# Ranks behind the second transposition, deviations on ScalarE, the first rows on its queue, weights issued sooner

## The reference, cut to what matters

```python
def _ln(v, axis, eps): return (v - mean(v, axis)) / sqrt(var(v, axis) + eps)

# x: (8 images, 64 channels, 16, 16); 256 positions per image
xn  = _ln(x, axis=1, eps=1e-6)
kq  = w_kq @ xn + b_kq                        # 32 channels
v   = w_v @ xn + b_v
att = softmax(kq.T @ kq, axis=-1)             # 256 x 256 per image
x   = x + w_o @ (att @ v) + b_o

t   = tokens(x)                               # 2048 tokens of 64
n   = _ln(t, axis=-1, eps=1e-5)
p   = softmax(n @ router_w.T)                 # 8 experts
top2 = top_k(p, 2), its two shares normalised to 1
y_e = (silu(n @ w1[e].T) * (n @ w3[e].T)) @ w2[e].T    # 682 hidden
out = t + sum over the two chosen experts of share * y_e
```

## Time and profile before

| | |
|---|---|
| three runs | 178.60, 179.76, 181.26 us |
| profiled execution | 177.17 us, span 175.4 us |
| busy, share of the span | PE 81%, PEld 68%, DVE 57%, ACT 41%, POOL 49% |
| granted TensorE clock, mean | 0.942 |
| DMA | 33.00 MB, 188 GB/s on average |
| largest lines | `up` 52.0 us of matmuls in each of its two rows, `down` 28.8 us, `multiply` 33.7 us, row scatters 31.4 us (32 of 980 ns), result scatters 37.7 us (39 of 967 ns) |

### The profile page before, as it was taken

One profiled execution on the slowest core, in us unless ns is written; L12 is line 12 of the kernel. 1 busy time (PEld: TensorE's weight loads), 2 busy tenths in 40 slices (PEclk: granted clock), 3 DMA queues, 4 the chain that ended last, 5 costly groups with the idle time before them and its releaser, 6 DMA issues.

```text
span 175.4 us, 4915 instructions
## 1 busy us (share of the span) xinstructions
PE 142.0 (81%) x1697; PEld 119.7 (68%) x1697; DVE 99.8 (57%) x372; ACT 71.2 (41%) x141; POOL 85.8 (49%) x114
## 2 busy tenths in 40 slices
PE   1489969590892596996699999999999999985672
PEld 1357746370561495895598999999999989874262
DVE  1626756858739857589357474637364736443050
ACT  2347664512430144262153545454545445443011
POOL 2695223877773772577653353525262626266000
PEclk9999999999579569999699999999999999999699
DMA  4999400001781692179697969596969881000345
GB/s 120 322 288 279 110 0 11 23 15 34 234 338 35 151 392 83 43 251 344 206 381 215 396 199 373 174 356 194 325 207 348 275 327 49 13 30 15 95 156 120
DMA packets 19893, 33.00 MB, mean 188 GB/s; under 512 B 7691, under 2 KB 13100, under 8 KB 19868
## 3 DMA queue, kind: packets, MB, share of 16 engines
q1 hardware_dynamic: 16732, 29.55, 52.1%
q0 software_dynamic: 2272, 2.35, 4.0%
q10 hardware_dynamic: 864, 0.79, 1.4%
HBM read 25.55 MB, written 7.13 MB: 186 GB/s over the span
## 4 chain that ended last, share of the span: by engine, by line
issue 31%; POOL 29%; PE 17%; DMA 8%; ACT 5%; DVE 5%; SPq 1%; POOLq 1%; ACTq 0%; DVEq 0%
POOL ys L383 20%; POOL xs L374 9%; PE psum L1055 4%; ACT probs L466 3%; DMA xs<-xrows,pos 2%; DMA y_in<-ys 2%; PE psum L1126 2%; PE psum L940 2%; PE psum L929 2%; PE psum L919 1%; DVE xrows L643 1%; DMA ys<-y_out,y_row 1%; DMA proj<-projections 1%; DMA x_in<-xs 1%; PE psum L1034 1%
## 5 line engine op out<-in xcount | busy, mean ns | idle before, releaser
L383 POOL DMA_INDIRECT ys<-y_out,y_row x39 | 37.7, 967 | 43.3 <-DVE y_out L848 34.1
L1055 PE MATMUL psum<-x_cols,weights 64*128 64x128 f32 x390 | 52.0, 288 | 3.5 <-DMA weights<-experts 3.3
L1055 PEld LDWEIGHTS psum<-x_cols,weights 64*128 64x128 f32 x390 | 48.1, 197 | 7.5 <-issue 5.4
L1057 PE MATMUL psum<-x_cols,weights 64*128 64x128 f32 x390 | 52.0, 288 | 0.0
L836 DVE TENSOR_TENSOR hid<-psum,act_sb 128x512 f32<-128x512 f32 (+1 forms) x50 | 33.7, 678 | 30.6 <-ACT act_sb L515 30.3
L1057 PEld LDWEIGHTS psum<-x_cols,weights 64*128 64x128 f32 x390 | 48.1, 197 | 0.0
L515 ACT ACTIVATE act_sb<-psum 128x512 f32<-128x512 f32 (+1 forms) x50 | 29.3, 586 | 29.8 <-PE psum L1055 29.8
L374 POOL DMA_INDIRECT xs<-xrows,pos x32 | 31.4, 980 | 18.4 <-DVE xrows L643 10.0
L1082 PE MATMUL psum<-hid,weights 128*64 128x128 f32 x468 | 28.8, 276 | 0.0
L1082 PEld LDWEIGHTS psum<-hid,weights 128*64 128x64 f32 x468 | 25.9, 137 | 1.8 <-DVE hid L836 0.3
L929 PE MATMUL psum<-ident,probs 128*128 128x128 f32 x32 | 6.6, 340 | 8.9 <-ACT probs L466 8.7
(11 more groups left out here) (150 smaller groups left out, 182.1 us busy)
## 6 DMA issues: line engine op xcount, KB each, us to landing
weights<-experts SPq DMA_DIRECT2D x39, 565.0 KB, 6.1
xs<-zeros SPq DMA_DIRECT2D x4, 1040.0 KB, 12.3
x_in<-xs SPq DMA_DIRECT2D x39, 32.5 KB
ys<-y_out,y_row POOLq DMA_INDIRECT x39
xs<-xrows,pos POOLq DMA_INDIRECT x32, 2.9
y_in<-ys ACTq DMA_DIRECT2D x2, 256.0 KB, 4.6
y_in<-ys SPq DMA_DIRECT2D x2, 256.0 KB, 4.3
x_sb<-x_tok SPq DMA_DIRECT2D x1, 384.0 KB, 3.6
```

Source lines behind the costliest of these rows:

```text
L383: nc.gpsimd.indirect_dma_start(ys, bass.IndirectOffsetOnAxis(ap=y_row[:, j:j + 1], axis=0), y_out[:, i % RING, h, :], None).then_inc(y_sca ...
L1055: first_ = nc.tensor.matmul(H1_BANK[g % 2][:, src], weights[0:C, slot, P * s:P * (s + 1)], x_cols[0:C, i % 2, src], start=True, stop=True)
L1057: second_ = nc.tensor.matmul(H3_BANK[g % 3][:, src], weights[C:P, slot, P * s:P * (s + 1)], x_cols[C:P, i % 2, src], start=True, stop=True)
```

## The change

- **Deviations.** POOL's two helpers go. ACT computes exp(-1/2 ln(variance + eps)) in two small activations, from a table set that has both functions: `inverse_deviations(k)` in two batches (pair 0; pairs 1 to 3 together) and `t_deviation(p)` for the second normalisation. DVE's first-half statistics are batched in the same way.
- **Ranks.** On PE `rank(p)` moves from behind `attend(2p+2)` and a fill of three to directly behind `transpose_probs(2p+3)`; on ACT both `exponentials` of a pair come ahead of the copies. The fills are resized (10 ahead of the last pair's transpositions, `keep_busy` 8 and 6 for 4 and 3).
- **First rows.** `load_rows(0)` and `load_rows(1)` are issued by ACT, behind its part of the first half and ahead of the last `t_deviation` and the load of the Silu table.
- **Weights.** SP issues the weights of quads 0 and 1 as soon as the first table is there, and those of quad 2 as soon as the second is there, ahead of the rows of quad 2.
- **Small moves.** `key_query(0)` goes ahead of one small product; `pair_up(0)` goes behind `positions(3)` and `used_up(0)`; `ones` is set by DVE. The `p >= 0` in `fill` changes nothing, as no negative p is passed.

```diff
             sp.wait_ge(table_ready, 1)
-            load_weights(0, owners_of(0))
-            early_rows, second_owners = [rows_of(0), rows_of(1)], owners_of(1)
-            landed(0)
-            load_rows(0, early_rows[0])
-            load_rows(1, early_rows[1])
-            load_weights(1, second_owners)
+            for i in quads_of(0):
+                load_weights(i, owners_of(i))
             for p in range(1, PHASES):
                 sp.wait_ge(table_ready, p + 1)
                 for i in quads_of(p):
-                    at = rows_of(i)
+                    if i < WQUADS:
+                        load_weights(i, owners_of(i))
+                for i in quads_of(p):
+                    at = rows_of(sp, i)
                     if i == quads_of(p)[0]:
-                        landed(p)
-                    load_rows(i, at)
-                    load_weights(i, owners_of(i))
+                        landed(sp, p)
+                    load_rows(sp, i, at)
+                    if i >= WQUADS:
+                        load_weights(i, owners_of(i))
...
+            def t_deviation(p):
+                act.wait_ge(moments_t_ready, p + 1)
+                nc.scalar.activation(logs[:, 1, pair(p)], moments_t[:, pair(p), 1], ACT.Ln, bias=eps[:, 1:2]
+                                     ).then_inc(logs_t_ready, 1)
+                act.wait_ge(logs_t_ready, p + 1)
+                nc.scalar.activation(rstd_t[:, pair(p)], logs[:, 1, pair(p)], ACT.Exp, scale=-0.5).then_inc(rstd_t_ready, 1)
...
                     normalise(p + 2)
                     xT_copy(p + 2)
+                exponentials(2 * p + 2)
                 u_copy(p + 1)
-                exponentials(2 * p + 2)
+                exponentials(2 * p + 3)
                 probsT_copy(2 * p + 2)
+                t_deviation(p)
                 if p + 2 < PAIRS:
                     kq_copy(p + 2)
-                exponentials(2 * p + 3)
                 probsT_copy(2 * p + 3)
+            act.wait_ge(table_ready, 1)
+            early_rows = [rows_of(act, i) for i in quads_of(0)]
+            landed(act, 0)
+            for i in quads_of(0):
+                load_rows(act, i, early_rows[i])
+            t_deviation(PAIRS - 1)
             nc.scalar.preload_act_table(ACT.Silu)
...
                 else:
                     normalise_t(p - 1)
-                    pair_up(0)
                 positions(p)
...
             used_up(0)
+            pair_up(0)
...
-                fill(p, 2)
+                fill(p, 2 if p < 2 else 10)
                 transpose_probs(2 * p + 2)
...
                 transpose_probs(2 * p + 3)
+                rank(p)
                 attend(2 * p + 2)
-                fill(p, 3)
-                rank(p)
+                fill(p + 1, 2)
             attend(B - 1)
-            keep_busy(4)
+            keep_busy(8)
             rank(PAIRS - 1)
-            keep_busy(3)
+            keep_busy(6)
```

More of the change, by code:

```diff
@@ L263, in all_scattered, with rows_of, load_rows, landed @@
                 engine.wait_ge(y_scattered[r], 16 * sum(len(members(i)) for i in range(r, NQ, RING)))
+        def rows_of(engine, i):
+            return [engine.value_load(table[0:1, 1, QUAD * i + h:QUAD * i + h + 1], min_val=0, max_val=E * CAP - SUB)
+                    for h in members(i)]
+        def load_rows(engine, i, at):
+            if i >= XRING:
+                engine.wait_ge(y_row_ready, i - XRING + 1)
+                engine.wait_ge(x_paired, i - XRING + 1)
+            for h in members(i):
+                engine.dma_start(x_in[:, i % XRING, h, :], xs[bass.ds(at[h], SUB), :]).then_inc(x_in_loaded[i % XRING], 16)
+        def landed(engine, p):
+            engine.wait_ge(dispatched[p], 16 * TPP * K_TOP * (KNOWN[p] - (KNOWN[p - 1] if p else 0)))
         def load_results(engine, q):
@@ L566, in chain, with x_statistics, scales @@
                 dve.wait_ge(dve_step, steps[0])
-            def x_statistics(p):
-                for t in range(TPP * p, TPP * (p + 1)):
+            def x_statistics(k):
+                for t in range(batch(k).start, batch(k).stop):
                     ins = nc.vector.bn_stats(parts[:, 0, t, :], x_sb[:, t, :])
                 chain(ins)
-                for t in range(TPP * p, TPP * (p + 1)):
+                for t in range(batch(k).start, batch(k).stop):
                     ins = nc.vector.bn_aggr(moments[:, t, :], parts[:, 0, t, :])
                 ins.then_inc(moments_ready, 1)
-            def scales(p):
-                dve.wait_ge(rstd_ready, p + 1)
-                nc.vector.scalar_tensor_tensor(out=shift_x[:, pair(p)], in0=moments[:, pair(p), 0], scalar=-1.0,
-                                               in1=rstd[:, pair(p)], op0=ALU.mult, op1=ALU.mult).then_inc(scale_ready, 1)
-                nc.vector.tensor_tensor(std[:, pair(p)], variance[:, pair(p)], rstd[:, pair(p)], ALU.mult
-                                        ).then_inc(scale_ready, 1)
+            def scales(k):
+                dve.wait_ge(rstd_ready, k + 1)
+                nc.vector.scalar_tensor_tensor(out=shift_x[:, batch(k)], in0=moments[:, batch(k), 0], scalar=-1.0,
+                                               in1=rstd[:, batch(k)], op0=ALU.mult, op1=ALU.mult).then_inc(scale_ready, 1)
+                nc.vector.scalar_tensor_tensor(out=std[:, batch(k)], in0=moments[:, batch(k), 1], scalar=EPS[0],
+                                               in1=rstd[:, batch(k)], op0=ALU.add, op1=ALU.mult).then_inc(scale_ready, 1)
             def x_logits(p):
@@ L753, in weigh @@
                                         ALU.mult).then_inc(gates_ready, 1)
+            nc.vector.memset(ones[:], 1.0).then_inc(ones_set, 1)
+            for k in range(2):
+                nc.vector.memset(eps[:, k:k + 1], EPS[k]).then_inc(eps_set, 1)
             nc.vector.memset(wu_x[:], 0.0).then_inc(rows_set, 1)
```

92 lines of the change are left out of this document (32 added, 60 removed).

## The result

Four runs of the changed kernel took 183.55 to 185.81 us, median 184.98. The kernel before, run four times beside it, took 179.41 (178.6 to 181.26). The ratio is 1.042 (95% interval 1.034 to 1.050). The forecast was 180.8 with a range up to 183.8, and "slower" had 0.16. It was wrong.

A forecast was written before the change was run, and what follows sets the result against it. Row scatters on GpSimd bound the kernel up to T, the expert half's start (60.34 us), then PE. T's shift of -1.5, +1.6 in quad 1 and +0.9 for SP's pace sum to +1.0: 179.76 becomes 180.8 us, range 176.4 to 183.8.

The forecast's parts named there:

- Term 2: First scatter: with the ranks moved, DVE's wait for the ranks of pair 0 goes, -2.6 us.
- Term 3: POOL without deviations: `t_deviation(1)` no longer sits between the scatters, -1.4 us.
- Term 5: Quad 1: PE's 3.30 us wait for quad 2's weights goes, but quad 2's rows come late behind them, +1.6 us.
- Term 1: The top: pair 0's deviation on ACT brings `normalise(1)` and `transpose_x(1)` sooner, -0.3 us.
- term 4: Landing beside flowing weights: +0.6 us for the last scatter and +2.2 us for the first rows.
- Rivals B: First rows pass the weights, so the 2.2 us of term 4 goes: 178.6 us, chance 0.23.
- rival D: First rows starve until both weight sets are through, landing behind 57.5; T does not move: 184.8 us, chance 0.14.
- term 6: SP's pace: later weight loads come late, a wait for weights in one of quads 6 to 8, +0.9 us.

The follow-up runs named there:

- e2: Changed kernel with all DMA issues as before; moved ranks, deviations on ACT and larger fills stay: 176.39 us, ratio 0.983.
- e6: Changed kernel with rows of quad 2 ahead of its weights, and weights of quad 1 issued only when the first scatters have landed: 181.9 us, ratio 1.018.
- e5: Changed kernel with `pair_up(3)` moved ahead of the third table's work on DVE: 183.51 us, ratio 1.028.
- e3: Changed kernel with idle matmuls at the tail, 14 ahead of the wait for the last result scatters and 20 instead of 10 behind: 182.22 us, ratio 1.024.
- e4: Kernel before with idle matmuls at the tail, 14 ahead of the wait for the last result scatters and 20 instead of 10 behind: 177.05 us, ratio 0.984.
- e11: Changed kernel with rows of quad 2 ahead of its weights, and weights of quad 1 issued only when the first rows have landed: 175.73 us, ratio 0.986.
- e16: Kernel before with only the DMA part of the change; ranks, deviations and fills as before: 187.82 us, ratio 1.049.
- e7: e2 with the ranks back behind `attend` and a fill of three: 176.26 us, ratio 0.988.
- e13: e2 with four table numbers read by one instruction, and the idle matmuls of e3 at the tail: 171.41 us, ratio 0.956.
- e15: Changed kernel with the weights of quad 1 issued only when the first rows have landed: 182.92 us, ratio 1.023.
- e14: e13 with the weights of quad 2 issued as soon as the second table is there, and its rows on GpSimd's queue: 174.86 us.
- e10: e7 with the idle matmuls of e3 at the tail: 175.5 us, ratio 0.989.
- e9: e2 with the idle matmuls of e3 at the tail: 172.55 us, ratio 0.973.

## Why the prediction was wrong

**Right.** Term 2: the 2.60 us wait is gone. Term 3: from the first scatter to the sixteenth it is 19.31 us against 20.67, the forecast 1.4 less. Term 5's mechanism in quad 1: `pair_up(2)` starts at T + 18.9 (forecast T + 19.3), quad 1 ends at T + 27.8 (T + 27.9), and PE's wait for the weights of quad 2 is gone.

**Short by 1.1 us: terms 1 and 2.** The last scatter moved by 3.2 us, not 4.3, and the shortfall is there at the first one: 1.85 sooner for 2.9. `place` started at 25.28 where 24.7 was forecast, without a wait. DVE, which before was free for it at 24.77, came free later, so what ends the wait for the ranks is DVE's own work. Term 1's 0.3 can't be told from chance: `place` starts between 24.19 and 26.10 in the thirteen kernels with this top.

**About the right sum from wrong parts: term 4.** It had +0.6 for the last scatter and +2.2 for the rows. Measured against the kernel before, the last scatter's landing cost 1.7 (5.95 against 4.21), and from the first issue of rows to T it was 0.5 more (7.23 against 6.70). e2, which has the same first half, gives the same: 1.7 for the landing and 0.3 for the rows (4.70 from first issue to copy, against 4.36). Rivals B and D both missed it: the rows neither pass the weights nor starve here, they come when the weights are nearly through. e6 shows the starving, with weights started beside the rows. Terms 1 and 2 lost 1.1 against the forecast and term 4 gave 0.5 back, so T moved by -0.9 where -1.5 was forecast.

**The failed step: term 5's exchange, +1.6, measured +3.2.** The prediction gave quad 2 9.3 us; it took 11.0. It counted PE's 3.30 us of waiting for weights as gained in full, but under those 3.30 us lay the third table's work on DVE, ahead of `pair_up(3)`. With the wait gone, that work itself held `turn_x(3)`. The prediction asks what each new wait will cost; it did not ask what other work the removed wait had covered. e5 takes the hold away and quad 2 is 9.43, though quad 1 took the gain back in that profile.

**Right by luck: term 6 and rival D.** Quads 3 to 9 took 0.9 us more, as forecast, but held by rows and not by weights (`pair_up` waits of 2.58, 1.74 and 1.95 us at 117, 126 and 135). Rival D's 184.8 is close to the measured 184.98, but its condition did not come: the first rows were copied at 56.87, not behind 57.5, and T did move.

**Not in the sum: the tail.** The sum ends where the experts end, and its +1.0 was carried to the time one for one. In the profiles the experts ended 3.1 later and the run 7.2; in the medians the run is 5.6 longer. The profile's 2.87 us of low clock on the last group were no term (before, the low clock lay under the idle matmuls, 3.76 us against 2.32), though PE's idle time ahead of them was in the trace. But e3 and e4, 5.2 us apart without it, say that it is chance rather than the change.

So of the 4.2 us between forecast and median, the expert part was missed by 2.1 in this profile and by 3.2 between e3 and e4. The rest is the tail and the spread from run to run, and the record does not part the two.

Beyond the forecast, the runs say what the DMA moves cost in all. With the rows of quad 2 first again (e1) the ratio goes from 1.042 to 0.997 and the median from 184.98 to 179.48. With the weights of quad 1 late as well (e11) they are 0.986 and 175.73. With the first rows back on SyncE (e2) they are 0.983 and 176.39, so ScalarE or SyncE makes no difference for them. The kernels ran on different chips and the medians contain the tail's chance, so the first step is shown well and the second roughly. e16 confirms the sign for the DMA part alone: +8.9 us.

## What to carry to other kernels

In this kernel big transfers belonged behind the small ones that somebody waits for, and "behind" meant until those had landed; another queue did not separate them. Before a wait is priced as gain, list what other engines do during it, since that work becomes the next wait. And where one queue's issuer runs as long per round as the engine it feeds, a gain ahead of it is handed back round by round, so lighten the issuer first.

## What the runs showed beyond that

- Quad 2 and quads 3 to 9 together took 75.53 us before, 75.57 in e1, 76.60 in e2 and 75.63 in e7: what quad 2 no longer waited for came back as waits for rows. e13, with a faster SyncE, took 73.06.
- An idle time of 3.8 to 6.1 us ahead of `up(9)` was followed by 7.4 to 8.9 us for work that takes 6.0 at the full clock (7.66 after, 7.42 e3, 8.19 e15, 8.67 e16, 8.77 e14, 8.91 e5). So the price of the low clock was 1.4 to 2.9 us, where the forecast had 1.6. In e10 an idle time of 1.57 us there cost next to nothing (6.12).
- The way of the results back (issue of `y_in` to the last group of matmuls) took 4.6 to 4.8 us in six kernels (before, e4, e9, e10, e14, e16) and 5.6 to 5.9 in the others, measured from SP's issue, for the same transfers and without regard to the clock. What decides that stays open.
